# Graph aggregation on one core: how the one-hot columns of the edge counts lie in memory

## The reference

```python
def sage(x, W_l, W_r, b):                    # mean over incoming edges
    agg = segment_sum(x[src], dst) / maximum(deg, 1)
    return agg @ W_l + x @ W_r + b
h = relu(sage(layernorm(x), W1_l, W1_r, b1))
x = x + sage(h, W2_l, W2_r, b2)
t = layernorm(x)                             # then 8 experts, top 2, gelu
x = x + t + sum_e combine[:, e] * (gelu(t @ w1[e] + b1[e]) @ w2[e] + b2[e])
```

## Time and profile before

| | us |
|---|---|
| median of 3 runs (657.53 to 657.73) | 657.7 |
| the profiled execution, timed | 658.81 |
| the span of its trace | 656.9 |
| TensorE busy | 570.9 |
| VectorE busy | 381.6 |
| ScalarE busy | 236.2 |
| GpSimd busy | 178.3 |

### The profile page before, as it was taken

The page is one execution under the profiler, slowest core; times in us unless marked ns, Lnnn a source line. Parts: engine busy times, 40 slices in busy tenths (PEclk is TensorE's granted clock), DMA queues, the critical chain, the costliest instruction groups (busy, mean ns, idle before and its releaser), DMA issues.

```text
span 656.9 us, 12332 instructions
## 1 busy us (share of the span) xinstructions
PE 570.9 (87%) x3085; PEld 336.5 (51%) x3086; DVE 381.6 (58%) x1304; ACT 236.2 (36%) x492; POOL 178.3 (27%) x171
## 2 busy tenths in 40 slices
PE   4986979999999999999999998899507999998870
PEld 2543445555555555554445454454205777777760
DVE  4876656666667666642656756657752554544440
ACT  4664834445444445421010000000003555645550
POOL 4533000000000000000213253344450565565660
PEclk9999989999999999999999999999757999999995
DMA  9321111111111111126313486632232675656656
GB/s 266 97 79 41 50 56 41 33 49 49 48 49 40 35 49 49 48 48 204 113 56 98 139 261 205 186 121 94 82 131 67 107 111 92 105 103 101 104 77 207
DMA packets 61952, 63.91 MB, mean 97 GB/s; under 512 B 9198, under 2 KB 59966, under 8 KB 61832
## 3 DMA queue, kind: packets, MB, share of 16 engines
q1 hardware_dynamic: 47880, 46.53, 23.5%
q0 software_dynamic: 10880, 14.66, 12.5%
q10 hardware_dynamic: 3152, 2.22, 1.2%
HBM read 35.77 MB, written 30.81 MB: 101 GB/s over the span
## 4 chain that ended last, share of the span: by engine, by line
PE 51%; DMA 16%; issue 13%; DVE 9%; POOL 6%; POOLq 2%; ACT 1%; SPq 0%; DVEq 0%; ACTq 0%
PE bank L1202 20%; DMA acc_dram<-adj 10%; PE counts_ps L614 6%; PE bank L1192 6%; PE bank L1123 6%; PE counts_ps L1202 4%; POOL xs_dram L549 3%; PE counts_ps L1351 3%; PE bank L1368 2%; DMA xs_dram<-onehots 2%; POOL stat L542 2%; DMA xs_dram<-w,onehots 2%; DMA y<-y_dram 1%; PE bank L1185 1%; POOLq L579 1%
## 5 line engine op out<-in xcount | busy, mean ns | idle before, releaser
L1202 PE MATMUL bank<-y,adj 128*128 128x512 f16 x625 | 155.7, 381 | 0.5 <-ACT zt L1421 0.5
L1202 PE MATMUL counts_ps<-y,adj 128*128 128x512 f16 x625 | 144.3, 379 | 2.0 <-DMA y<-y_dram 2.0
L621 ACT ACTIVATE adj<-counts_ps 128x1000 f32 (+1 forms) x80 | 80.2, 1004 | 64.3 <-PE counts_ps L614 64.3
L585 POOL DMA_INDIRECT acc_dram<-adj x52 | 80.8, 1553 | 73.1 <-ACT adj L1555 38.7
L1202 PEld LDWEIGHTS counts_ps<-y,adj 128*128 128x128 f16 x625 | 60.7, 101 | 64.8 <-DMA y<-y_dram 3.9
L1202 PEld LDWEIGHTS bank<-y,adj 128*128 128x128 f16 x625 | 58.2, 98 | 60.1 <-issue 14.8
L1351 PE MATMUL counts_ps<-adj 128*128 x224 | 57.1, 399 | 5.5 <-ACT adj L1531 5.4
L530 POOL IOTA onehots<- 128x8 int32 x1 | 0.1, 143 | 223.9 <-PE counts_ps L614 223.9
L614 PEld LDWEIGHTS counts_ps<-onehots 125*128 125x128 f16 x640 | 41.3, 98 | 30.1 <-issue 14.0
L1368 PE MATMUL bank<-adj 128*128 x208 | 51.7, 388 | 5.0 <-DVE adj L1084 3.1
L614 PE MATMUL counts_ps<-onehots 125*128 125x125 f16 x640 | 51.4, 222 | 5.2 <-DVE onehots L600 5.2
(11 more groups left out here) (222 smaller groups left out, 702.1 us busy)
## 6 DMA issues: line engine op xcount, KB each, us to landing
adj<-xs_dram SPq DMA_DIRECT2D x56, 132.0 KB, 2.6
rows<-z_dram SPq DMA_DIRECT2D x49, 128.0 KB, 2.1
z_dram<-zt SPq DMA_DIRECT2D x36, 128.0 KB, 1.7
adj<-in_L_ffn_w SPq DMA_DIRECT2D x16, 256.0 KB, 3.2
acc_dram<-yo SPq DMA_DIRECT2D x25, 128.0 KB, 1.9
rows<-in_x SPq DMA_DIRECT2D x24, 128.0 KB
y_dram<-yo SPq DMA_DIRECT2D x23, 128.0 KB, 1.7
y<-y_dram SPq DMA_DIRECT2D x4, 640.0 KB, 6.7
```

The lines of the kernel that those rows point to most:

```text
L585: g.indirect_dma_start(acc_dram, bass.IndirectOffsetOnAxis(ap=ids[s][h], axis=0), ye[s][h], None, compute_op=ALU.add).then_inc(ye_out[s][h ...
L621: nc.scalar.activation(adj[:, :, bass.ds(at, GW * WD)].rearrange("p b (h d) -> p b h d", d=WD), counts_ps[:, 2 * (group % 2):2 * (group % ...
L1202: last = te.matmul(to, adj[:, b, t * P:(t + 1) * P], y[:, b, :], start=(b == 0), stop=(b == NT - 1))
```

## The change

One constant is set from 2 to 1. A pair of windows becomes a single window: its 128 (or 125) columns stand side by side, `iota_4` holds each number once, the comparison walks over columns innermost while the edge's own number is repeated, and a matmul takes adjacent elements. Numbers of instructions, elements, waits and transfers are as before.

```diff
     GW = 8
-    HALF = 2
+    HALF = 1
     OF_BANK = 4
```

## The result

| | before | after |
|---|---|---|
| median, us | 657.7 (657.5 to 659.4, 4 runs) | 715.8 (713.9 to 717.5, 4 runs) |
| span of the profiled execution, us | 656.9 | 713.0 |
| TensorE busy, us | 570.9 | 578.7 |
| VectorE busy, us | 381.6 | 461.8 |

The ratio is 1.087, with a 95% interval of 1.083 to 1.090. The forecast was 720 us, in a range of 706 to 734.

A forecast was written before the change was run, and what follows sets the result against it. It took a serial loop between TensorE's aggregate and VectorE's comparisons to bound the first aggregation. Growth of 57.2 us in tiles 2 to 22 plus 5.2 before gave a 719.3 us span, forecast 720 us, range 706 to 734.

The forecast's parts named there:

- The comparison's price: VectorE's L600 comparisons go from 684 and 674 ns to 1218 and 1191, 84 us over 80 pairs.
- The loop: First aggregation: aggregate ends, hidden rows, comparisons, counts, rest of aggregate; three-group tiles 8.89 to 11.49 us, four-group 9.37 to 12.65.
- the tail: TensorE work from a tile's last group load to the next hidden rows: 2.91 us, or 1.83 with four groups.
- Before tile 2: Start, tile 0 and tile 1 grow by 2.2, 1.05 and 1.97 us, together 5.2.
- Part (b): L614 matmuls read adjacent weights and moving columns: nothing expected, at most 0.06 us per group, 5 us over 80.
- Two per cycle survives: Rival, 5%: L600 comparisons stay at 684 ns and only adjacent reading counts, 654 to 658 us.
- VectorE has room: Rival, 4%: VectorE's work can slide, so only four-group tiles and the start pay, 667 us.
- The clock falls: Rival, 6%: waiting TensorE drops to 1.2 GHz, 5.7 us more per tile; 850 us for all tiles, 785 for half.
- A different slow price: Rival, 3%: one comparison of the pair stays fast, +1.10 us fewer per pair, about 690 us.
- TensorE goes on the moment the comparison is ready: First aggregation: groups one and two load weights 0.79 us after the second comparison's start, so TensorE waits twice a tile.

The follow-up runs named there:

- The single comparisons: Kernel before plus nine two-source and four single-source comparisons behind line 796: 0.69 us all dense, 1.22 to 1.23 with a repeated or step-two source, 1.30 with step-two output.
- the slow comparison alone: Kernel before with comparisons walking columns innermost, edge number repeated, tables still interleaved and matmuls reading every second element: 729.0 us, ratio 1.106.
- the reordered kernel: Kernel before (HALF = 2) with the next tile's first pair made on VectorE ahead of the wait for the aggregate: 653.8 us, ratio 0.993.

## Why the prediction was right

**The comparison's price.** 1218 and 1191 ns were forecast, 1218 and 1195 came. I had taken the upper bound from one row whose two sources were both unusual, so it could not say which of them had the price. The single comparisons show that either has all of it, and that the choice was right.

**The loop.** The period's terms hold one by one in the rows of the tile after: hidden rows 0.92 (218.78 to 219.70), pair 2.24 (219.70 to 221.94), load 1.31 behind the second comparison, all three groups decided by VectorE. 

**The step that was mis-sized: the tail.** I took the time from the last load to the next hidden rows, 2.91 us (1.83 with four groups), out of the trace of before. After the change it is 230.06 - 227.35 = 2.71 (2.70 by most tiles; 242.50 - 240.88 = 1.62 with four groups). Before, TensorE was still at its matmuls when the load was issued, 0.22 us ahead of its own matmul (load 196.25):

```profile
196.47 0.64 PE L614 MATMUL counts_ps<-onehots 125*128 125x125 f16 x8
```

A TensorE that has run dry starts the matmul 0.03 behind the load (222.14, 222.17). I measured from a load that had run ahead. So the tile is 11.28 and not 11.49, 12.44 and not 12.65: 21 x 0.21 = 4.4 us of the 6.3 us by which the forecast span (719.3 against 713.0) was too long.

**Before tile 2.** From the first pair to the next step after tile 0 the forecast growth was 2.2 + 1.05 = 3.25 and the measured one 31.28 - 28.10 = 3.18 (93.11 - 61.83, against 91.55 - 63.45). Tile 1 took 10.56 instead of 10.76, the same tail. The first pair itself started at 61.83 us and not at 63.45, 1.6 us that I hadn't in the sum. It isn't the change's: in the eight profiled kernels whose path to it is the same the first pair starts between 61.83 and 64.29 us, with fast and slow comparisons mixed. These make the 6.3 (4.4 + 0.2 + 1.6, and 0.1).

The medians are closer, 720 against 715.8, and part of that is luck: I put the median 0.8 us above the profiled span, and after the change it lies 2.8 above.

**Part (b).** Forecast as nothing, with a bound of 60 less 52 ns per matmul. Measured 0.02 us for a group's eight (0.64 to 0.62 us), a third of the bound, and all of it from the moving columns. The weight loads stayed at 98 ns. The Trainium skill, "SBUF — State Buffer", section "Door 1: The DMA port swizzle", has steps of up to eight 2-byte elements for free; TensorE's reads at step two here cost nearly nothing, 0.02 us in 0.64; larger steps were not tried.

**The rivals.** *Two per cycle survives* is out by the 1.22 us. *VectorE has room* was wrong for this order and right as a mechanism: in another order the kernel after takes 669 us, where I had 667 for it. *The clock falls* did not come true after the change, although TensorE was busy for only 79 to 82% of a tile: the granted clock is 1.00 in both tiles shown and over the whole stretch from 101 to 343 us. In small it did in the two kernels with one table side by side and in the slow comparison alone: their tile 1 ran at 0.84 to 0.85. *A different slow price*, one comparison staying fast, I had mispriced: the kernels of that kind took 681 us and not about 690, since a slow comparison adds 0.52 us to a pair and not 1.10.

**What I read too strongly.** "TensorE goes on the moment the comparison is ready" was right, but the wait behind it was 0.13 us a tile, as the reordered kernel shows. It told where the loop would close once a pair grew, not that much was lost already.

**Open.** Why the comparison onto interleaved tables took 1341 ns in the kernel and 1.30 us by itself. The two differ in the ramp too: step two in the kernel, step one in the single comparison. And the 80 in the kernel were not alike: 1281 to 1443 ns, the longest of them among the seven groups of phase 1. It wasn't tried whether other engines' accesses make the difference. Open too is why tile 1 ran at a clock of 0.84 to 0.85 in those three kernels, and at 1.00 before and after the change.

## What to carry to other kernels

Before a layout is made simpler for the reader of a table, price what the writer loses: in a comparison of two 2-byte sources an innermost step of zero or two cost VectorE half its rate here (1.22 against 0.69 us for 1024 elements), and an inner run of two was enough to keep it. A producer with a fifth of its time free (VectorE, 8.76 of 11.28 us busy) can still be on the path, if it stands behind a wait in its own program order; look at the distance from its last instruction to the consumer's first, not at its busy share. And a distance read from a saturated engine is not the one that holds when it has run dry.

## What the runs showed of the hardware that was not expected

An output with a step of two on 2-byte data costs more than a source with one: 1.30 against 1.22 us for 1024 elements, and 1341 ns inside the kernel. Reading every second 2-byte element as moving columns costs TensorE 0.02 us in eight matmuls of 125 columns; as weights it costs nothing that the traces show. A single-source comparison of 128 elements takes 0.25 us, and four of them start 0.16 us apart.
